# Parameter loads one chunk sooner, and the feed-forward block's last products a step sooner

## The chip, the core and the metric

The kernel runs on one core of a Trainium2 chip. The metric is the device time of one launch in microseconds. TensorE (PE in the rows, its weight loads PEld), VectorE (DVE), ScalarE (ACT) and GpSimd (POOL) each run their own instruction list in order; SyncE (SP) issues the DMAs. They meet at semaphores only.

## What is computed

Input x is 2048 tokens of 128 features. An attention layer, then a stack S0 of six layers, then a second attention layer, then the same stack again as S1 (same weights), each with a layer norm in front and added back to x. The change touches only the stacks:

```python
for i in range(DEPTH):                      # DEPTH = 6
    x = attn_layer(shift_tokens(x), Wqkv[i], q_scale[i], k_scale[i], Wo[i]) + x
    x = ffn_layer(shift_tokens(x), ln_g[i], ln_b[i], W1[i], b1[i], W2[i], b2[i]) + x

def ffn_layer(x, g, bln, W1, b1, W2, b2):
    xn = (x - mu) / jnp.sqrt(var + 1e-05) * g + bln
    hg = xn @ W1 + b1                       # W1: 128 x 682
    a, gate = jnp.split(hg, 2, -1)          # value and gate, 341 wide each
    return a * jax.nn.gelu(gate) @ W2 + b2  # W2: 341 x 128
```

`attn_layer` is attention over windows of 32 tokens with 16 heads of 64, normed and rotated queries and keys.

## The kernel before, in words

**Chunks, blocks, steps.** A stack cuts the 2048 tokens into 16 chunks of 128 (`NCH`). The feed-forward part works on blocks of 4 chunks (512 tokens, `NB` = 4 a layer). Every engine runs the same list of steps (`read_steps`): 16 steps for layer 0, a loop of 16 steps over layers 1 to 5, and a few steps that drain the pipeline (11 on PE, 12 on DVE). In step k an engine works on chunk k-d for several distances d: `at.chunk(d)`. `at.block(d)` gives block (k-d)//4 if (k-d) mod 4 is 3, so each piece of feed-forward work comes once in four steps. Steps with k beyond the layer reach back into the layer before. Each engine has its own step count: what DVE does with a chunk in its step k+2 answers what PE did with it in its step k. Below, "PE step 0, 1, 2, 3" is k mod 4 on PE.

**PE's step.** In this order: attention's output product (L602), transposition of the probabilities (L542), the query projection (L535 to L537) into `slot[0]`, probabilities times values (L681), scores (L704, L711) into `slot[3]`, transposition of the queries into `slot[2]` after `wait_for_slot2`, value projection, transposition of the attention output, key projection, transposition of the keys. Between them stands the feed-forward work of a block: mean (L669, `block(4)`, PE step 3), variance (L572, `block(5)`, step 0), the spread of the inverse deviation (L591, `block(6)`, step 1), three gate products (L546, `block(7)`, step 2), three value products (L546; `block(8)` in step 3, `block(9)` in step 0, `block(10)` in step 1) and the second product with W2 (L646, `block(11)`, step 2, ahead of the query projection). Value tile 1 lands in the half of `slot[2]` that the query transposition takes next, the second product in the half of `slot[3]` that the scores take next.

**The others.** ACT copies PE's outputs out of the slots and takes the Gelu of the gates (L862). DVE applies bias and gate to each value product (`hide`, L1155: three a block, by distances 9, 10, 11), does the norm's product (L1075, distance 7, which waits for all value products of the block before) and adds the second product, its bias and the residual into `XA` (L1118, distance 12, semaphore `f_done`). POOL does half of the rotation and the powers (L929, L913, L942, L946).

**Loads.** The stack's weights have one buffer each. SP's `layer` walks over the chunks c; per chunk it issues ten copies of the value windows (`window_values`, L456 to L460), which wait until ACT has copied the values of chunk c. Ahead of `window_values` of certain chunks it loads one parameter of this layer, after a wait that says that the layer before is through with the old one: `Wo` at c = 3, the rotation scales at 5, the norm's columns at 7, gate bias at 8, `W1` at 9, value bias at 10, `W2` at 11, `b2` at 12. Layers 1 to 5 of both stacks do this, ten times in all. The semaphores `wo_in`, `w1_in`, `value_b_in` release PE's L602 in step 4, PE's L546 in step 10 and DVE's first L1155.

Of the kernel before, what the change touches and what calls it, by code (L numbers as in the profile page):

```python
# [32 lines left out]
START = 1  # L33
# [57 lines left out]
def build(nc, A, out, place, stages=("A", "S0", "B", "S1")):  # L91
    n_const = A["shape_constants"].shape[1]
    ctx = ExitStack()
    with ctx:
# [153 lines left out]
        s = {n: sem(n) for n in names}  # L248
# [149 lines left out]
        def sp_stack(sp, call):  # L398
# [64 lines left out]
            def layer(L, following, after):  # L463
                first = isinstance(L, int) and L == 0
                g, f = L * NCH + CHUNKS * call, L * NB + BLOCKS * call
                t = (L + DEPTH * call) * 3
                if following is not None:
                    sp.wait_ge(s["w_lo_done"], START + t + 3)
                    load_q(following)
                for c in range(NCH):  # L470
                    if c == NCH - 1 and following is not None:
                        sp.wait_ge(s["w_lo_done"], START + t + 4)
                        load_v(following)
                        if after is not None:
                            sp.wait_ge(s["w_lo_done"], START + t + 5)
                            load_k(after)
                    if c == 3 and not first:
                        sp.wait_ge(s["y_mm"], START + g)
                        load_wo(L)
                    if c == 5:  # L480
                        sp.wait_ge(s["tables_done"], START + TABLES * call + 4 + 16 * L)
                        load_scales(0 if following is None else following)
                    if c == 7 and not first:
                        sp.wait_ge(s["ln_done"], START + norms_before(call) + f)
                        load_cols(L)
                    if c == 8 and not first:
                        sp.wait_ge(s["gelu_done"], START + 3 * f)
                        load_b1(L, 1)
                    if c == 9 and not first:
                        sp.wait_ge(s["value_mm"], START + 3 * f)  # L490
                        load_w1(L)
                    if c == 10 and not first:
                        sp.wait_ge(s["hid_done"], START + 3 * f)
                        load_b1(L, 0)
                    if c == 11 and not first:
                        sp.wait_ge(s["w2_mm"], START + f)
                        load_w2(L)
                    if c == 12 and not first:
                        sp.wait_ge(s["f_done"], START + 2 * f)
                        load_b2(L)  # L500
                    window_values(g, c)
# [25 lines left out]
        def pe_stack(pe, call):  # L527
            n0 = norms_before(call)
# [19 lines left out]
            def step(layer, g, f, k, lo, hi):  # L548
# [4 lines left out]
                def wait_for_slot2():  # L553
                    pe.wait_ge(s["ot_sb"], START + upto(k - 4))
                    pe.wait_ge(s["xb_done"], START + 2 * upto(k - 4))
                    if at.block(7) is not None:
                        pe.wait_ge(s["gelu_done"], START + 3 * blocks(k - 7))
                    if at.block(9) is not None:
                        pe.wait_ge(s["hid_done"], START + 3 * blocks(k - 9) - 1)
                    if at.block(10) is not None:  # L560
                        pe.wait_ge(s["hid_done"], START + 3 * blocks(k - 10))
                    if at.block(4) is not None:
                        pe.wait_ge(s["ln_centred"], START + n0 + blocks(k - 4))

# [71 lines left out]
                        pe.wait_ge(s["hid_done"], START + 3 * blocks(k - 11))  # L636
                    first_layer(slot[2][0:FT[2][1], 512:1024], 1, *FFN_TILES[2]).then_inc(s["gate_mm"], 1)

                b = at.block(11)
                if b is not None:  # L640
                    if b % NB == 0:
                        pe.wait_ge(s["w2_in"], START + 48 * (layer + DEPTH * call + b // NB + 1))
                    pe.wait_ge(s["hid_done"], START + 3 * (f + b + 1))
                    pe.wait_ge(s["sub_done"], START + upto(k - 3))
                    for t, (j, a, m) in enumerate(VALUE_TILES):
                        mm = pe.matmul(slot[3][:, 512:1024], W2[0:m, j, :], hidden[0:m, j, :],  # L646
                                       start=(t == 0), stop=(t == 2))
                    mm.then_inc(s["w2_mm"], 1)
# [7 lines left out]
                    pe.wait_ge(s["ak_done"], START + upto(c - 1))  # L656
                    project_in(slot[0], c % 4, 0).then_inc(s["q_mm"], 1)

                b = at.block(10)
                if b is not None:  # L660
                    pe.wait_ge(s["xb_done"], START + 2 * upto(k - 4))
                    if draining:
# [25 lines left out]
                if c is not None:  # L688
                    pe.wait_ge(s["qT_sb"], START + g + c + 1)
                    pe.wait_ge(s["kT_sb"], START + g + c + 1)  # L690
                    pe.wait_ge(s["sub_done"], START + upto(c - 1))
                    if at.block(5) is not None:
                        pe.wait_ge(s["ln_eps"], START + n0 + blocks(k - 5))
                    if at.block(6) is not None:
                        pe.wait_ge(s["ln_half"], START + n0 + blocks(k - 6))
                    if at.block(7) is not None:
                        pe.wait_ge(s["gelu_done"], START + 3 * blocks(k - 7))
                    if at.block(11) is not None:
                        pe.wait_ge(s["f_done"], START + 2 * blocks(k - 11))
                    if at.block(8) is not None:  # L700
                        pe.wait_ge(s["hid_done"], START + 3 * blocks(k - 8) - 2)
                    first = 0 if c % NCH == 0 else 1
                    for i in range(2):
                        pe.matmul(slot[3][:, i * 512:(i + 1) * 512], ident_b[:, :],  # L704
                                  mask_win[:, first:first + 1, :].to_broadcast([128, 8, 2 * WIN]),
                                  start=True, stop=False, skip_group_check=True)
                    for h in range(H):
                        r = 64 * (h % 2)
                        col = (h % 2) * 512 + (h // 2) * 64
                        for w in range(4):  # L710
                            mm = pe.matmul(slot[3][32 * w:32 * w + 32, col:col + 64],  # L711
                                           qT[r:r + 64, h // 2, 32 * w:32 * w + 32],
                                           kT[r:r + 64, h // 2, 32 * w:32 * w + 64],
                                           start=False, stop=True, skip_group_check=True)
                    mm.then_inc(s["s_mm"], 1)
# [35 lines left out]
                        pe.wait_ge(s["on_done"], START + upto(k - 3))  # L751
                    turn(slot[1], rot_out[1]).then_inc(s["tk_mm"], 1)

            read_steps(pe, call, step, 11)

        def act_stack(act, call):
            n0 = norms_before(call)
# [219 lines left out]
        def dve_stack(dve, call):  # L977
# [20 lines left out]
            def step(layer, g, f, k, lo, hi):  # L998
# [108 lines left out]
                    dve.tensor_tensor(rot_out[1][:, :], rot_out[1][:, :], rot_sin[1], ALU.add)\  # L1107
                       .then_inc(s["rk_done"], 1)

                b = at.block(12)  # L1110
                if b is not None:
                    if b % NB == 0:
                        dve.wait_ge(s["b2_in"], START + 16 * (layer + DEPTH * call + b // NB + 1))
# [10 lines left out]
                    dve.wait_ge(s["iq_done"], START + g + c + 1)  # L1124
                    normalise(0, "qn_done")

                b = at.block(11)
                if b is not None:
                    hide(layer, f, b, 2)

# [29 lines left out]
            for i, name in enumerate(names_of):  # L1160
# [1 line left out]
                                  const(name).rearrange("p (c d) -> p c d", d=DH),  # L1162
                                  qk_scales[:, i:i + 1, :].to_broadcast([128, NCH, DH]), ALU.mult)\
                   .then_inc(s["tables_done"], 1)
            read_steps(dve, call, step, 12)

            for b in range(NB):
                dve.wait_ge(s["f_done"], START + 2 * (BLOCKS * (call + 1) - NB + b + 1))
# [957 lines left out]
```

## Time and profile before

| | us |
|---|---|
| Time, median of 3 runs (7095.42 to 7106.72) | 7104.73 |
| The profiled execution's own time | 7119.09 |
| Its span | 7117.3 |
| Stack S0, first to last key copy of ACT (L821) | 1064.5 to 2984.9 |
| Stack S1, the same | 5129.3 to 7033.0 |

The profiled execution is 14.4 us above the median. Both stacks together are some 54% of the span. In the rows a line number is that of the kernel shown above, times are microseconds from the span's start, and an idle time in brackets is what the engine waited just before the group of instructions, with the instruction or DMA that ended the wait. One instruction serves as a marker of steps below: ACT's copy of the key projection, L821, once a step. From one L821 to the next is one step's length. Names of tiles that share memory are mixed in the rows: `W` is W1 or W2, `b` is a bias of the first product, and `normed<-slot,b,centred` is `hide`.

### The profile page before, as it was taken

How to read it: one execution, taken by the hardware profiler on the slowest of the kernel's cores; microseconds unless marked ns; L12 is line 12 of the kernel's file. 1: busy time of each engine (PE TensorE's matmuls, PEld its weight loads, DVE VectorE, ACT ScalarE, POOL GpSimd, SP SyncE). 2: the span in 40 equal slices, each digit the busy share in tenths (PEclk: the TensorE clock that was granted, in tenths of full speed). 3: DMA queues.
4: the chain of work that ended last, by engine and by line, in shares of the span. 5: the costliest groups of instructions: out<-in, count | busy, mean ns of one | idle time of the engine just before them, and what ended most of it. 6: DMA issues, size and time to landing. Idle time of an engine off the chain costs nothing. (4 is left out here: it accounts for less than half of the span.)

```text
span 7117.3 us, 188486 instructions
## 1 busy us (share of the span) xinstructions
PE 6050.2 (85%) x75387; PEld 4080.9 (57%) x75387; DVE 4642.6 (65%) x5380; ACT 3318.6 (47%) x3775; POOL 4252.9 (60%) x2000
## 2 busy tenths in 40 slices
PE   8989878888888888889889889999688888888887
PEld 4334436666666666655555555555376666666665
DVE  5425528887878887775455445543388787878776
ACT  1342246665656555513333333333366565656554
POOL 0000008777777777616567666667787777777764
PEclk6665569999999999989989989999899999999999
DMA  0000002222222222200000000000122222222221
GB/s 23 1 2 1 1 22 62 67 59 62 59 62 59 64 60 59 53 8 1 1 2 1 1 2 1 1 1 1 31 64 65 57 68 54 67 65 61 57 56 49
DMA packets 187287, 254.59 MB, mean 36 GB/s; under 512 B 59996, under 2 KB 80984, under 8 KB 186200
## 3 DMA queue, kind: packets, MB, share of 16 engines
q1 hardware_dynamic: 186392, 242.02, 13.1%
q8 instruction: 639, 10.47, 0.6%
q14 instruction: 256, 2.10, 0.1%
HBM read 38.98 MB, written 1.57 MB: 6 GB/s over the span
## 5 line engine op out<-in xcount | busy, mean ns | idle before, releaser
L1813 POOL TENSOR_TENSOR XB<-XB,Pb 128x1024 f32<-128x1024 f32 x448 | 1079.3, 2409 | 290.3 <-ACT Pb L1771 265.1
L913 POOL TENSOR_TENSOR sin_qk<-raw_qk,rot 128x512 f32<-128x512 f32 x768 | 1008.9, 1334 | 188.7 <-ACT raw_qk L875 133.1
L1865 DVE TENSOR_REDUCE b_pmax<-slot 128x1 f32<-128x1024 f32 x512 | 621.2, 1223 | 611.5 <-PE slot L1607 611.3
L1771 ACT ACTIVATE Pb<-slot 128x1024 f32<-128x1024 f32 x512 | 504.5, 1024 | 951.7 <-PE slot L1634 880.5
L946 POOL TENSOR_TENSOR inv_norm<-norm2c,minus_half 128x16 f32<-128x16 f32 x192 | 678.2, 3532 | 386.9 <-DVE norm2c L1088 386.9
L929 POOL TENSOR_TENSOR rot_out<-rot_out,sin_qk 128x1024 f32<-128x1024 f32 x192 | 601.2, 3131 | 337.7 <-DVE rot_out L987 336.6
L286 POOL TENSOR_TENSOR rstd<-variance,minus_half 128x4 f32<-128x4 f32 x20 | 19.8, 1008 | 1075.6 <-DVE variance L295 1075.5
L535 PE MATMUL slot<-w_hi,x_hi 128*128 128x512 f32 x1152 | 538.2, 467 | 73.5 <-POOL w_lo L904 43.4
L786 ACT ACTIVATE qT<-slot 128x1024 f32<-128x1024 f32 x192 | 197.1, 1026 | 794.3 <-PE slot L542 794.3
L942 POOL TENSOR_TENSOR inv_norm<-norm2c,minus_half 128x16 f32<-128x16 f32 x192 | 559.0, 2912 | 0.0
L987 DVE TENSOR_TENSOR rot_out<-slot,rot 128x1024 f32<-128x1024 f32 x384 | 467.9, 1219 | 83.5 <-PE slot L542 42.6
L711 PE MATMUL slot<-kT,qT 64*32 64x64 f32 x24576 | 334.6, 229 | 218.4 <-issue 218.3
L1644 PE MATMUL slot<-Pb,Vb 128*64 128x512 f32 x2048 | 494.3, 604 | 1.1 <-ACT Pb L1771 1.1
L542 PE MATMUL slot<-consts,rot_out 128*128 128x128 f32 x3072 | 435.1, 287 | 69.3 <-issue 39.5
L991 DVE TENSOR_TENSOR rot_out<-rot_out,inv_norm 128x1024 f32<-128x1024 f32 x384 | 474.9, 1237 | 6.8 <-POOL inv_norm L942 5.3
L602 PE MATMUL slot<-OT,Wo 128*128 128x128 f32 x3072 | 404.9, 288 | 82.7 <-DMA Wo<-in_Wo 80.0
L536 PE MATMUL slot<-w_lo,x_hi 128*128 128x512 f32 x1152 | 471.4, 409 | 2.6 <-issue 2.6
L537 PE MATMUL slot<-w_hi,x_lo 128*128 128x512 f32 x1152 | 469.6, 408 | 0.0
L711 PEld LDWEIGHTS slot<-kT,qT 64*32 64x32 f32 x24576 | 274.1, 107 | 325.9 <-issue 325.9
L602 PEld LDWEIGHTS slot<-OT,Wo 128*128 128x128 f32 x3072 | 386.5, 203 | 106.7 <-issue 101.8
L542 PEld LDWEIGHTS slot<-consts,rot_out 128*128 128x128 f32 x3072 | 363.8, 147 | 137.7 <-issue 84.0
L1632 PE MATMUL slot<-QA,KA 128*128 128x512 f32 x1024 | 423.6, 414 | 11.3 <-ACT Pb L1771 7.5
(223 smaller groups left out, 13525.8 us busy)
## 6 DMA issues: line engine op xcount, KB each, us to landing
VW<-V SPq DMA_DIRECT2D x1152, 128.0 KB
VW<-V SPq DMA_DIRECT2D x768, 64.0 KB
w_raw<-in_Wqkv SPq DMA_DIRECT2D x36, 512.0 KB, 3.6
Wo<-in_Wo SPq DMA_DIRECT2D x12, 512.0 KB, 4.1
W<-in_W SPq DMA_DIRECT2D x12, 341.0 KB, 3.1
consts<-in_shape_constants SPq DMA_DIRECT2D x1, 2436.5 KB, 8.7
W<-in_W SPq DMA_DIRECT2D x24, 64.0 KB
out<-out_nat SPq DMA_DIRECT2D x2, 512.0 KB, 3.4
```

The source lines that it names most:

```text
L535: pe.matmul(out, x_hi[ring][:, :], w_hi[:, cols], start=True, stop=False)
L542: mm = pe.transpose(o[:, j * 128:(j + 1) * 128], src[:, j * 128:(j + 1) * 128], ident)
L602: mm = pe.matmul(slot[2][:, 512:640], Wo[:, j, :], OT[:, j, :], start=(j == 0), stop=(j == 7))
L711: mm = pe.matmul(slot[3][32 * w:32 * w + 32, col:col + 64], qT[r:r + 64, h // 2, 32 * w:32 * w + 32], kT[r:r + 64, h // 2, 32 * w:32 * w + ...
L913: ins = pool.tensor_tensor(dst[:, :, x, :], src[:, :, 1 - x, :], tab, ALU.mult)
L929: pool.tensor_tensor(rot_out[0][:, :], rot_out[0][:, :], rot_sin[0], ALU.add)\
L942: pool.tensor_tensor(inv_norm[0][:, :], norm2c[0][:, :], minus_half[:, 0:H], ALU.pow)\
L946: pool.tensor_tensor(inv_norm[1][:, :], norm2c[1][:, :], minus_half[:, 0:H], ALU.pow)\
L1644: mm = pe.matmul(slot[3][64 * hh:64 * hh + 64, 0:512], Vb[:, k, :], Pb[:, n % B_RING, 512 * hh:512 * hh + 512], start=(k == 0), stop=(k == ...
L1771: act.activation(Pb[:, n % B_RING, :], slot[n % 2][:, :], ACT.Exp).then_inc(s["b_exp"], 1)
L1813: pool.tensor_tensor(b_sum[:, qb % 2, :], Pb[:, (n - 1) % B_RING, :] if k == 1 else b_sum[:, qb % 2, :], Pb[:, n % B_RING, :], ALU.add).th ...
L1865: dve.tensor_reduce(b_pmax[:, n // 2, n % 2:n % 2 + 1], o[:, :], AX.X, ALU.max).then_inc(s["b_max"], 1)
```

## The change

Every load of a layer's parameters moves one chunk up in SP's list. The value product of tile 1 moves from PE step 1 to PE step 0 of its block, with its `hide` on DVE one step sooner. The second product moves from PE step 2 to step 1, `f_done` one DVE step sooner. The waits of the slots follow. Both engines drain in one step less. No instruction is added or removed inside the layers; one wait is joined with another in `wait_for_slot2`, and one is added for the drain alone.

```diff
-                    if c == 3 and not first:
+                    if c == 2 and not first:
                         sp.wait_ge(s["y_mm"], START + g)
                         load_wo(L)
-                    if c == 5:
+                    if c == 4:
 ...                                             # scales
-                    if c == 7 and not first:
+                    if c == 6 and not first:
 ...                                             # norm columns; gate bias 8 -> 7
-                    if c == 9 and not first:
+                    if c == 8 and not first:
                         sp.wait_ge(s["value_mm"], START + 3 * f)
                         load_w1(L)
-                    if c == 10 and not first:
+                    if c == 9 and not first:
                         sp.wait_ge(s["hid_done"], START + 3 * f)
                         load_b1(L, 0)
-                    if c == 11 and not first:
+                    if c == 10 and not first:
                         sp.wait_ge(s["w2_mm"], START + f)
                         load_w2(L)
-                    if c == 12 and not first:
+                    if c == 11 and not first:
                         sp.wait_ge(s["f_done"], START + 2 * f)
                         load_b2(L)
@@ pe: wait_for_slot2
                     if at.block(9) is not None:
-                        pe.wait_ge(s["hid_done"], START + 3 * blocks(k - 9) - 1)
-                    if at.block(10) is not None:
-                        pe.wait_ge(s["hid_done"], START + 3 * blocks(k - 10))
+                        pe.wait_ge(s["hid_done"], START + 3 * blocks(k - 9))
@@ pe: second product
-                b = at.block(11)
+                b = at.block(10)
                 if b is not None:
+                    if draining:
+                        pe.wait_ge(s["ln_eps"], START + n0 + blocks(k - 6))
@@ pe: value product of tile 1
-                b = at.block(10)
+                b = at.block(9)
@@ pe: before the scores
-                    if at.block(11) is not None:
-                        pe.wait_ge(s["f_done"], START + 2 * blocks(k - 11))
+                    if at.block(10) is not None:
+                        pe.wait_ge(s["f_done"], START + 2 * blocks(k - 10))
-            read_steps(pe, call, step, 11)
+            read_steps(pe, call, step, 10)
@@ dve: f_done
-                b = at.block(12)
+                b = at.block(11)
@@ dve: third hide
-                b = at.block(11)
+                b = at.block(10)
                 if b is not None:
                     hide(layer, f, b, 2)
-            read_steps(dve, call, step, 12)
+            read_steps(dve, call, step, 11)
```

## Rows read from the trace of the kernel before

**Rows 1.** The page, part 1: busy time, share, instructions of each engine.

```profile
PE 6050.2 (85%) x75387; PEld 4080.9 (57%) x75387; DVE 4642.6 (65%) x5380; ACT 3318.6 (47%) x3775; POOL 4252.9 (60%) x2000
```

**Rows 2.** Waits, whole span: waiter <- releaser: us in total, times, longest.

```profile
PE slot L602 <- DMA Wo<-in_Wo: 80.0, 10, 8.2
PE slot L546 <- DMA W<-in_W: 60.8, 10, 6.3
DVE normed L1155 <- DMA b<-in_b: 40.6, 10, 4.5
DVE normed L1075 <- PE slot L546: 100.3, 46, 3.2
```

**Rows 3.** Timeline of SP's DMA issues, one layer: start, us, what.

```profile
2057.45 0.60 SPq L460 DMA_DIRECT2D VW<-V  x1
...
2078.84 0.40 SPq L422 DMA_DIRECT2D Wo<-in_Wo  x1
...
2199.74 0.59 SPq L460 DMA_DIRECT2D VW<-V  x1
...
2200.61 0.36 SPq L426 DMA_DIRECT2D W<-in_W  x1
...
2228.64 1.36 SPq L436 DMA_DIRECT2D b<-in_b  x3
```

**Rows 4.** Windows by step: length, busy (count) per engine, granted clock, DMA; sums.

```profile
sum 77.30, PE 55.06 PEld 41.09 DVE 50.12 ACT 37.19 POOL 45.63; mean PE 18.35 PEld 13.70 DVE 16.71 ACT 12.40 POOL 15.21
...
sum 59.90, PE 52.23 PEld 40.35 DVE 50.85 ACT 37.34 POOL 45.88; mean PE 17.41 PEld 13.45 DVE 16.95 ACT 12.45 POOL 15.29
...
6127.70:6155.10 27.40, 18.13 (x337) 14.63 (x336) 16.55 (x21) 10.62 (x13) 16.52 (x9) 0.81 0.22 60
...
sum 78.90, PE 55.23 PEld 41.49 DVE 49.47 ACT 37.20 POOL 44.60; mean PE 18.41 PEld 13.83 DVE 16.49 ACT 12.40 POOL 14.87
...
6211.10:6228.40 17.30, 15.44 (x337) 12.50 (x336) 16.50 (x21) 10.70 (x13) 15.93 (x9) 1.00 0.26 64
...
sum 55.80, PE 49.71 PEld 37.97 DVE 51.39 ACT 37.28 POOL 45.70; mean PE 16.57 PEld 12.66 DVE 17.13 ACT 12.43 POOL 15.23
```

**Rows 5.** Timeline of PE, output product after the wait for Wo, and in another step.

```profile
2082.83 3.78 PE L602 MATMUL slot<-OT,Wo 128*128 128x128 f32 x16 [7.88 <-DMA Wo<-in_Wo]
...
2179.14 1.95 PE L602 MATMUL slot<-OT,Wo 128*128 128x128 f32 x16
```

**Rows 6.** Timeline of PE in a PE step 1.

```profile
2183.45 1.02 PE L546 MATMUL slot<-normed,W 128*128 128x512 f32 x2
...
2189.77 1.09 PE L542 MATMUL slot<-consts,rot_out 128*128 128x128 f32 x8 [0.27 <-DVE normed L1155]
2191.10 0.50 PE L535 MATMUL slot<-w_hi,x_hi 128*128 128x512 f32 x1 [0.24 <-DVE Os L1142]
```

**Rows 7.** Timeline of a PE step 2: PE's second product and scores, ACT's Gelu.

```profile
2124.52 2.74 PE L646 MATMUL slot<-normed,W 128*128 128x512 f32 x6
2126.70 0.79 PE L535 MATMUL slot<-w_hi,x_hi 128*128 128x512 f32 x1
...
2130.28 0.60 PE L704 MATMUL slot<-mask_win,ident_b 128*128 128x512 bf16 x2 [0.21 <-issue]
...
2126.11 1.83 ACT L862 ACTIVATE centred<-slot,b 128x512 f32<-128x512 f32 x3
```

**Rows 8.** Timeline of a PE step 0: DVE's query normalisation, PE's query transposition.

```profile
2254.88 1.24 DVE L991 TENSOR_TENSOR rot_out<-rot_out,inv_norm 128x1024 f32<-128x1024 f32 x1
...
2257.60 1.09 PE L542 MATMUL slot<-consts,rot_out 128*128 128x128 f32 x8 [0.17 <-issue]
```

**Rows 9.** Timeline of the first stack's drain, DVE and PE.

```profile
3044.41 1.53 DVE L1118 SCALAR_TENSOR_TENSOR XA<-slot,ffn_cols,XB 64x512 f32<-64x512 f32 x2 [5.70 <-PE slot L646]
...
3046.09 2.81 PE L546 MATMUL slot<-normed,W 128*128 128x512 f32 x6 [1.72 <-DVE XA L1118]
```

**Rows 10.** View of one line, L1134: durations in ns, least, median, most.

```profile
L1134 DVE TENSOR_TENSOR x_lo<-XA,x_hi x192: 273/280/2332, 1053.7 to 7007.0; 128x128 fp32r<-128x128 f32 x192
```

More of the change, by code:

```diff
@@ L476, in layer @@
                             load_k(after)
-                    if c == 3 and not first:
+                    if c == 2 and not first:
                         sp.wait_ge(s["y_mm"], START + g)
                         load_wo(L)
-                    if c == 5:
+                    if c == 4:
                         sp.wait_ge(s["tables_done"], START + TABLES * call + 4 + 16 * L)
                         load_scales(0 if following is None else following)
-                    if c == 7 and not first:
+                    if c == 6 and not first:
                         sp.wait_ge(s["ln_done"], START + norms_before(call) + f)
                         load_cols(L)
-                    if c == 8 and not first:
+                    if c == 7 and not first:
                         sp.wait_ge(s["gelu_done"], START + 3 * f)
                         load_b1(L, 1)
-                    if c == 9 and not first:
+                    if c == 8 and not first:
                         sp.wait_ge(s["value_mm"], START + 3 * f)
                         load_w1(L)
-                    if c == 10 and not first:
+                    if c == 9 and not first:
                         sp.wait_ge(s["hid_done"], START + 3 * f)
                         load_b1(L, 0)
-                    if c == 11 and not first:
+                    if c == 10 and not first:
                         sp.wait_ge(s["w2_mm"], START + f)
                         load_w2(L)
-                    if c == 12 and not first:
+                    if c == 11 and not first:
                         sp.wait_ge(s["f_done"], START + 2 * f)
```

## The prediction

> **What bounds the kernel now.** I read the page first. PE is the busiest engine, 85% of the span [rows 1], but that is an average over stages, and the change touches only the stacks. So I read the waits next: who stands idle there, and what ends it. Three of the waits end on a DMA, and each comes exactly ten times, once for each layer that reloads its parameters: PE waits 80.0 us in all for `Wo`, 60.8 us for `W1`, and DVE 40.6 us for the value bias [rows 2]. A fourth wait of interest ends on PE: DVE's norm product waits 100.3 us for the value product of the block before [rows 2], 2.2 us in each of 46 blocks.
>
> Is it the issue or the transfer that is late? SP's timeline tells. `Wo` is issued at 2078.84 [rows 3], and PE's output product starts at 2082.83, after 7.88 us of idle time [rows 5]: 4.0 us from issue to use, so PE had stood still since 2074.95, before the load was even issued. SP could not issue sooner because the load stands behind the ten window copies of the chunk before, which in turn wait for that chunk's values. The same holds for `W1` (issued 2200.61) and the value bias (issued 2228.64) [rows 3].
>
> Then I ask what a step costs without the wait. The windows view, cut at ACT's L821, gives each step's length. I take the three steps with a DMA wait in one layer of each stack, and three steps of the same layer that do the same work (the same k mod 4, none with a wait for a load). First stack: 77.3 against 59.9 us, 17.4 us apart. Second stack: 78.9 against 55.8 us, 23.1 us apart [rows 4]. DVE and POOL are busy for about the same time in both (50.1 and 50.9 us DVE in the first pair), so the longer steps hold waiting, not work. In a clean step of 17.3 us PE is busy for 15.4, DVE for 16.5 and POOL for 15.9 us [rows 4]: three engines close to full. That is why I expect nothing below that length.
>
> **The loads, one chunk sooner.** No instruction is added. Each load now goes out behind the windows of a chunk earlier. For `Wo` that is right after 2057.45 + 0.60 = 2058.1 [rows 3], 20.8 us sooner, against 7.88 us that are missing. `W1` would go out one step sooner, 17.3 us if the step is a clean one [rows 4], against 60.8/10 = 6.1 us missing. The value bias takes the place that `W1` has now, 28.0 us sooner [rows 3], against 4.1 us. All three waits go, with over 10 us to spare.
>
> What each wait on SP holds up: behind it stand the ten window copies of the next chunk, and behind those PE's L681. But these copies wait for the values of the next chunk in any case, which PE makes late in the following step, and what the loads wait for has happened by then: each of the old parameters is last read in the step in which SP gets there or before, since `value_mm`, `hid_done`, `w2_mm` and `f_done` themselves come a step sooner. I take 0 for this; if one wait held SP, it would have to hold it for over 10 us before PE saw it.
>
> What comes back: the whole difference between the pairs of steps, since that is measured between steps with and without the wait. Mean (17.4 + 23.1)/2 = 20.25 us a layer, times 10: **-202 us**, with 174 and 231 us as bounds. It is more than PE's idle time, and a row shows why. After the wait for `Wo` the sixteen matmuls of L602 take 3.78 us, otherwise 1.95 us [rows 5], and the granted clock of that kind of step is 0.81 on average against 1.00 in the clean one [rows 4]: for part of the step PE runs at the lower of its two levels (1.2 instead of 2.4 GHz) right after having been idle. So a removed wait also takes the slow matmuls behind it away.
>
> The Trainium skill, "TensorE: Matmul & The Clock Gate", Part 1, puts it so: the throttled state is the default and activity releases it. By this the extra is part of the gain. If it were not, only the waits themselves would return, some 18.1 us a layer and 181 us in all; the clock in the rows agrees with the page.
>
> **The feed-forward products, a step sooner.** Work only moves, so I price each of four PE steps by what comes and goes. A value product costs 1.02 us (L546 x2) [rows 6]. The second product takes from 2124.52 to 2126.70, and the matmul behind it takes 0.79 instead of 0.50 us [rows 6, 7], which gives 2.18 + 0.29 = 2.47 us.
>
> - PE step 0 gains the value product: **+1.02**. New wait: the query transposition now also needs the third `hide`, 0.75 us of DVE, which stands right behind DVE's query normalisation. In the rows that normalisation ends at 2256.12 and PE gets to the transposition at 2257.60 [rows 8], so `hide` ends at 2256.9 and costs nothing. Without this cover it would cost 0.75 us, and behind it in PE's list is all the rest of the step.
> - PE step 1 gains the second product and loses the value product, +2.47 - 1.02. The `hide` that left it had PE wait 0.27 us, and the attention output behind it 0.24 us more [rows 6]; both go: **+0.94**. New wait: the scores now need `f_done` here, 1.53 us of DVE [rows 9] ahead of the query normalisation. It can start when the second product is done; PE has the query projection and L681 (some 3 us) to do meanwhile, so I take 0. DVE's step grows by 1.53 and shrinks by 0.75 and by the 2.2 us wait for the value product.
> - PE step 2 loses the second product. PE then gets to the scores 2.47 us sooner, but they also wait for the Gelus, which end at 2126.11 + 1.83 = 2127.94, against 2130.28 now [rows 7]: **-2.34**. What is late next there is ACT, then DVE, which loses `f_done` in this step.
> - PE step 3: nothing.
>
> Sum -0.38 us for four steps, times 46 blocks: **-17 us**. Bounds: if the `hide` wait is paid in full and nothing of step 1's waits returns, +1.77 + 1.45 - 2.34 = +0.88, times 46 = +40 us. If the added work fills waits that PE has anyway in steps 0 and 1 (it is busy for 15.4 us of the 17.3 us of a clean step [rows 4], so there are 1.9 us to fill), only the -2.34 stays: -108 us. I take the middle value, as its terms are read from rows of the very steps.
>
> **The drain.** In the last steps of a stack PE's value products wait 1.72 us for DVE's `f_done` of the block before, which waited for the second product [rows 9]. That product now lies ahead of the gates. About 2 us a stack: **-4 us**; between 0 and -5.7 each, the idle time of DVE there.
>
> **Sum.** -202 - 17 - 4 = -223 us. Against the profiled execution's own 7119.1 us that is 6896 us. It lies 14.4 us above the median, so the median should be 7104.7 - 223 = **6881 us**.
>
> **The rivals.**
> 1. *The waits go, but less comes back* (0.15). Another engine is late where the load was. For it: in the first stack's pair the clean steps are no shorter than 59.9 us, and three engines are nearly full. Price: 174 back, +40 for the products, -4: -138, so 6967 us.
> 2. *The products bring more* (0.08). DVE's wait of 100.3 us goes from a path on which POOL waits for it: -231 - 108 - 4 = -343, so 6762 us. Against it: PE has more to do in that very step.
> 3. *DVE and POOL collide more often* (0.06). DVE's 128x128 subtraction L1134 takes 0.28 us as a rule and up to 2.33 us [rows 10], although nothing in it changes. If the new order adds (0.28 + 2.33)/2 - 0.28 = 1.0 us of this in two steps of each block, 2 x 46 x 1.0 = 94 us are lost: 6975 us. The Trainium skill, "SBUF — State Buffer", names a cause: a port pair shared by VectorE and GpSimd, held by one of them for a whole instruction. The rows show the long durations, not the cause.
> 4. *Slower* (0.04). The moved work lies in series on both engines and step 2 gives nothing back: the PE work and the DVE work each lengthen their steps, 2.47 + 1.02 + 0.75 + 1.53 = 5.77 us a block, times 46 = 265 us against 206 us of loads and drain: +59, so 7164 us. The place is PE's wait for `f_done` ahead of the scores in step 1. It decides from 206/46 = 4.5 us a block on. Against it: rows 7 and 8 show cover for two of the four terms.
> 5. *It does not do what it says* (0.03): SP gets to the loads sooner, but is held there until the old time. Only the drain moves: 7101 us, no change. Against it: the copies ahead of `W1` end at 2199.74 + 0.59 = 2200.33, and it follows at 2200.61 [rows 3], so the place in SP's list decides, not the semaphore.
>
> **How the numbers follow.** The forecast has 0.60; its own range is 6840 to 6935 us (174 to 231 us of loads, and half of the way to the bounds of the products). The remaining 0.04 is for gains of another size. The range that should hold the time 8 times in 10 takes in the forecast and rivals 1 and 3: 6825 to 6985 us. Differences below 0.2% (14 us) can't be told from none here. Faster: 0.60 + 0.15 + 0.08 + 0.06 + 0.04 = 0.93. Same: 0.03. Slower: 0.04.
>
> **What would show it.** The three DMA waits of rows 2 gone from the list, and the steps that held them as long as their like, near 17, 21 and 18 to 22 us. L602 near 1.95 us in each step 4. A second product in PE step 1, with that step about 1 us longer and PE step 2 over 2 us shorter. DVE's L1075 without its wait. Wrong would be: a long wait of PE's L704 for L1118 (rival 4), or of L542 for L1155 in PE step 0 (rival 1), an SP wait ahead of a load (rival 5), or steps with the load now bound by POOL or DVE at over 20 us.

## The result and the profile after

The changed kernel takes 6796.92 us (median of 4 runs, 6793.93 to 6798.29) against 7101.05 us of the kernel before beside it. The ratio is 0.9571 with a 95% interval of 0.9555 to 0.9588: 304 us or 4.3% faster. 223 us were forecast, with a range of 6825 to 6985 us. The direction is right; the gain is 81 us larger, and the time lies 28 us below the range.

The page of the changed kernel, the row that answers to [rows 1], and two of the page's groups of instructions:

```profile
PE 5957.6 (88%) x75387; PEld 4031.7 (59%) x75387; DVE 4574.7 (67%) x5380; ACT 3310.4 (49%) x3775; POOL 4234.6 (62%) x2000
...
L946 POOL TENSOR_TENSOR inv_norm<-norm2c,minus_half 128x16 f32<-128x16 f32 x192 | 668.9, 3484 | 171.4 <-DVE norm2c L1088 171.1
...
L600 PE MATMUL slot<-OT,Wo 128*128 128x128 f32 x3072 | 389.5, 281 | 2.7 <-ACT OT L814 2.7
```

The counts are the same. PE has 92.6 us less busy time with the same 75387 matmuls: some of them ran faster, as matmuls behind a long wait had been slow [rows 5]. The output product alone went from 404.9 to 389.5 us. It is now L600 and waits for nothing but 2.7 us of ACT, where 80.0 us stood [rows 2]. DVE's wait of 100.3 us for the value product [rows 2] is gone from the list of waits, and its wait for the second product went from 157.8 to 14.3 us. POOL's wait for DVE at L946 was 386.9 us in the page of before and is 171.1 now.

SP's timeline in the layer of [rows 3]:

```profile
1983.17 0.59 SPq L460 DMA_DIRECT2D VW<-V  x1
1984.04 0.40 SPq L422 DMA_DIRECT2D Wo<-in_Wo  x1
...
2096.15 0.36 SPq L426 DMA_DIRECT2D W<-in_W  x1
```

The windows of the three steps that held a wait for a load (length, busy per engine, granted clock, DMA share, GB/s), and their sum:

```profile
1998.90:2015.30 16.40, 15.96 (x339) 12.83 (x338) 15.54 (x21) 10.66 (x13) 15.38 (x9) 1.00 0.25 66
2108.10:2126.20 18.10, 16.09 (x333) 12.39 (x332) 14.29 (x18) 13.66 (x17) 14.67 (x8) 1.00 0.25 61
2126.20:2145.10 18.90, 15.46 (x331) 12.03 (x329) 16.67 (x22) 12.91 (x16) 14.05 (x8) 1.00 0.26 67
...
sum 53.40, PE 47.51 PEld 37.25 DVE 46.51 ACT 37.24 POOL 44.09; mean PE 15.84 PEld 12.42 DVE 15.50 ACT 12.41 POOL 14.70
```

`Wo` goes out 0.3 us after the last window copy, so SP holds it for nothing. The three steps are 53.4 us long instead of 77.3 [rows 4], at the full clock.

To see where the rest came from I take the distance between the L821 markers in every step, as a mean over layers 1 to 5 of both stacks, and group the sixteen steps of a layer by PE's k mod 4. The distance from marker i to marker i+1 holds PE step i+1; behind the last marker of a stack there is none, so the step that begins a layer is a mean of eight and not of ten. All values in the table below come so from the trace of the kernel named, in us a step:

| kernel | PE step 0 | PE step 1 | PE step 2 | PE step 3 | a block | time to before |
|---|---|---|---|---|---|---|
| before | 21.75 | 18.17 | 22.90 | 20.04 | 82.9 | 1 |
| all loads sooner | 19.28 | 18.85 | 20.40 | 19.25 | 77.8 | 0.9718 |
| loads, value product | 19.25 | 18.03 | 20.16 | 19.16 | 76.6 | 0.9639 |
| the whole change | 19.30 | 19.23 | 17.96 | 19.06 | 75.5 | 0.9576 |

(The last two rows are of runs e12 and e15 below, which ran on one chip.) The loads shorten PE step 0 (`Wo`), PE step 2 (`W1`) and PE step 3 (the value bias). The products shorten step 2 and lengthen step 1 by little.

### The profile page after: what moved, and what is told of

Its sections match the earlier page's. It is cut to its first block and busy times, and to the rows that moved or that the text cites. A ratio compares the mean times of both kernels' runs of the same rounds, so it can differ in the third digit from the quotient of the medians.

```text
span 6792.1 us, 188444 instructions
## 1 busy us (share of the span) xinstructions
PE 5957.6 (88%) x75387; PEld 4031.7 (59%) x75387; DVE 4574.7 (67%) x5380; ACT 3310.4 (49%) x3775; POOL 4234.6 (62%) x2000
## 5 line engine op out<-in xcount | busy, mean ns | idle before, releaser
L946 POOL TENSOR_TENSOR inv_norm<-norm2c,minus_half 128x16 f32<-128x16 f32 x192 | 668.9, 3484 | 171.4 <-DVE norm2c L1088 171.1
L711 PE MATMUL slot<-kT,qT 64*32 64x64 f32 x24576 | 333.1, 228 | 182.0 <-issue 181.8
L1634 PE MATMUL slot<-QB,KB 66*128 66x512 f32 x1024 | 416.3, 407 | 0.0
L600 PE MATMUL slot<-OT,Wo 128*128 128x128 f32 x3072 | 389.5, 281 | 2.7 <-ACT OT L814 2.7
```

The source lines that it names most:

```text
L600: mm = pe.matmul(slot[2][:, 512:640], Wo[:, j, :], OT[:, j, :], start=(j == 0), stop=(j == 7))
L711: mm = pe.matmul(slot[3][32 * w:32 * w + 32, col:col + 64], qT[r:r + 64, h // 2, 32 * w:32 * w + 32], kT[r:r + 64, h // 2, 32 * w:32 * w + ...
L946: pool.tensor_tensor(inv_norm[1][:, :], norm2c[1][:, :], minus_half[:, 0:H], ALU.pow)\
```

## The experiments

**Loads or products.** All eight loads alone, the products alone, the value product alone, and `Wo` alone.

```diff
 e1_loads: all eight "if c == n" lines as in the change, nothing else
 e2_products: all of the change but the loads
 e3_value:
-                b = at.block(10)          # pe: value product of tile 1
+                b = at.block(9)
-                b = at.block(11)          # dve: third hide
+                b = at.block(10)
 e4_wo:
-                    if c == 3 and not first:
+                    if c == 2 and not first:
                         sp.wait_ge(s["y_mm"], START + g)
                         load_wo(L)
```

> The kernel before with all eight loads a chunk sooner and nothing else. The whole change took 304 us off. Theory A, the sum on record: the loads bring 202 us (bounds 174 and 231), so about 6899 us. Theory B: the loads bring nearly all of it, 280 us or more, about 6820 us or less, because a wait for a load held back more steps than the one in which it stood. Either way the three DMA waits are gone.

Measured: 6927.14 us, ratio 0.9718 (0.9702 to 0.9735), which is 200 us off. Theory A holds to 2 us, theory B falls. In the markers the three steps that had waited are 22.8 us a layer shorter, more than the 20.25 us forecast, and the other thirteen are 2.5 us longer; 2.7 us of this is the step after marker 4. SP now waits in one place, 11.6 us in all and 1.7 us at most, ahead of `W1`.

> The kernel before with the load of Wo alone a chunk sooner. By the pairs of steps on record (10.4 us in the first stack, 10.1 us in the second) 102 us, about 6999 us. By the bare wait of the trace, 80 us, about 7021 us. If more than the one step gains, over 110 us.

Measured: 7028.69 us, ratio 0.9862 (0.9844 to 0.9879), 98 us off. The pairs of steps had priced it at 102 us, the bare wait at 80 us, which lies outside the interval (86 us at its near end). The pair method is the better one.

> The kernel before with the value product, the third hide, the second product and the addition a step sooner, and the loads where they were. The sum on record gives 21 us (17 + 4), so about 7080 us. Theory C: the products bring some 100 us, about 7000 us, because DVE's wait of 100.3 us for the value product was on a path that POOL waited for. Theory B says 7080 us or more.

Measured: 7055.03 us, ratio 0.9888 (0.9867 to 0.9909), 80 us off. The sum on record (21 us) is refuted; theory C's 100 us are nearer, though the next run shows that its reason carries only a part. Together with the loads the products bring more still: 0.9718 to 0.9571, 104 us.

> The kernel before with the value product of tile 1 and its hide alone a step sooner; second product, addition and loads stay. It takes away DVE's wait for the value product (100.3 us) with no other work moved. Theory C: some 100 us faster, about 7000 us. The sum on record, by its terms: PE step 0 gains 1.02, step 1 loses 1.02 + 0.27 + 0.24, so 0.5 us a block or 23 us faster, about 7078 us.

Measured: 7066.01 us, ratio 0.9918 (0.9902 to 0.9935), 58 us off, between the two theories (23 and 100 us). The step that the value product left, PE step 1, is 1.1 us shorter (18.17 to 17.04 us), the one that took it in 0.2 us longer.

**Where a product on PE is free.** To price PE work by itself I added products of constants whose result is overwritten.

```diff
 e7_dummy0: loads sooner, and in PE step 0 behind the query projection
+                b = at.block(9)
+                if b is not None:
+                    pe.wait_ge(s["xb_done"], START + 2 * upto(k - 4))
+                    pe.matmul(slot[2][:, 512:1024], const("centre128"), const("rot_q_cos")[:, 0:512],
+                              start=True, stop=True)
 e11_dummy0_late: the same product behind the scores
                     wait_for_slot2()
+                    if at.block(9) is not None:
+                        pe.matmul(slot[2][:, 512:1024], ...)
                     turn(slot[2], rot_out[0]).then_inc(s["tq_mm"], 1)
 e8_dummy1: loads sooner, and in PE step 1 ahead of the query projection
+                b = at.block(10)
+                if b is not None and not draining:
+                    pe.wait_ge(s["sub_done"], START + upto(k - 3))
+                    for t in range(3):
+                        pe.matmul(slot[3][:, 512:1024], ...)
```

> The kernel with all loads sooner (0.9718 of before) and one more product of 128x512 on PE in step 0 of every block, at the place that the value product moves to; it multiplies constants and its result is overwritten. The price on record is 1.02 us a block in full, 47 us: 0.9784. Theory D, such work is hidden in step 0: 0 to 15 us, 0.9718 to 0.974.

Measured: 6910.52 us, ratio 0.9703 (0.9679 to 0.9727). The product costs nothing in PE step 0 (19.26 us against 19.28 without it); 1.02 us a block had been charged, 0.9784, which lies outside the interval.

> All loads sooner and one more product of 128x512 in PE step 0, as in the run in which it cost nothing (0.9703 against 0.9718 without it), but behind the scores instead of ahead of them. Theory H: ahead of L681 and L711 the product fills time in which PE would have stood still inside these two groups for no wait that the profile shows (1.9 us a step without it, 1.1 us with it); behind them it can't, and costs 0.86 to 1.02 us a block, 40 to 47 us: 0.977 to 0.978. Rival: the step is bound by DVE and POOL, and the product is free at either place: 0.970 to 0.973.

Measured: 6945.47 us, ratio 0.9759 (0.9743 to 0.9776). The same product some 6 us later in the same step costs 0.56% more than ahead (40 us, though the two ran on different chips). Against no product it costs 0.41%, 29 us, or 0.66 us in PE step 0; theory H had charged 40 to 47 us, which the intervals don't rule out. Being free hangs on the place. The timeline of PE in the same step of the same layer shows it, first without the product, then with it ahead (L662), then with it behind (L722):

```profile
6078.34 1.66 PE L681 MATMUL slot<-VW,probsT 64*32 64x64 f32 x128
6080.05 0.60 PE L704 MATMUL slot<-mask_win,ident_b 128*128 128x512 bf16 x2
6080.58 1.12 PE L711 MATMUL slot<-kT,qT 64*32 64x64 f32 x91
6083.88 0.63 PE L711 MATMUL slot<-kT,qT 64*32 64x64 f32 x37 [2.18 <-issue]
```

```profile
6082.20 1.02 PE L662 MATMUL slot<-consts 128*128 128x512 f32 x2
6083.15 1.48 PE L687 MATMUL slot<-VW,probsT 64*32 64x64 f32 x128
6084.72 0.60 PE L710 MATMUL slot<-mask_win,ident_b 128*128 128x512 bf16 x2
6085.26 0.84 PE L717 MATMUL slot<-kT,qT 64*32 64x64 f32 x63
6087.22 0.86 PE L717 MATMUL slot<-kT,qT 64*32 64x64 f32 x65 [1.12 <-issue]
```

```profile
6088.46 1.61 PE L681 MATMUL slot<-VW,probsT 64*32 64x64 f32 x128
...
6093.43 0.78 PE L711 MATMUL slot<-kT,qT 64*32 64x64 f32 x55 [1.78 <-issue]
6094.33 1.12 PE L722 MATMUL slot<-consts 128*128 128x512 f32 x2
```

"Issue" marks idle time in which PE waits for nothing that the profile shows. It stands in the middle of the 128 short matmuls of the scores. From the start of the values' product (L681, L687) to the end of the scores it is 6.17 us without the extra product and 4.93 us with it ahead: 1.24 us shorter, more than the 0.95 us that the product takes up in PE's row. As a mean over the 30 such steps that don't begin a layer it is 5.73 us without the product, 4.78 us with it ahead and 5.27 us with it behind. The last value warns: up to the end of the scores e11 has the same instructions as e1, and yet is 0.46 us shorter, so not all of the 0.95 us is the product's doing.

The same 30 steps show what gave way. With the product ahead PE is busy for 0.43 us more, not 0.95, while the mean granted clock rises from 0.97 to 1.00, so the other matmuls ran a little faster; and PE is idle for 0.63 us less. With the product behind, it is 0.76 us more and 0.30 us less. The prediction's bound of -108 us had this as added work that "fills waits that PE has anyway".

What PE stands still for inside these groups can be read from the DMA packets in the trace. Queue 8 carries packets of 16384 bytes of the kind "instruction"; the page of e1 has them as

```profile
q8 instruction: 639, 10.47, 0.7%
```

In e1 PE stands still 182 times for over 0.6 us inside the values' product or the scores. In 180 of these it goes on 1.2 to 1.6 us after such a packet has landed, 1.38 us in the median; of random moments in the stacks 6% lie so. In the three stops above the packet lands at 6082.39, 6085.72 and 6092.01, and PE goes on at 6083.88, 6087.22 and 6093.43. So PE waits for its instructions there. In the first of them the packet sets out 0.4 us after the scores have begun, in the second, with the product ahead, 0.5 us before. What decides when a packet sets out was not tested.

> The kernel with all loads sooner and three more products of 128x512 on PE in step 1, ahead of the query projection, where the second product moves to; results overwritten, none in the drain. In full 2.47 us a block for 44 blocks: 109 us, 0.987. Theory D, partly hidden: 1.2 to 2.0 us a block, 53 to 88 us, 0.979 to 0.984.

Measured: 7013.64 us, ratio 0.9854 (0.9824 to 0.9884), 97 us more than without, above theory D's 53 to 88 us but by less than the intervals. In PE step 1 the work is nearly paid in full, 2.2 of 2.47 us, although it stands ahead of the short matmuls here too: being ahead of them is not enough. Two rows from the waits of this kernel say how it travels; the same two of the kernel with the loads alone follow:

```profile
DVE normed L1082 <- PE slot L546: 212.1, 46, 5.3
POOL inv_norm L953 <- DVE norm2c L1095: 356.0, 153, 6.5
```

```profile
DVE normed L1075 <- PE slot L546: 97.8, 46, 2.8
POOL inv_norm L946 <- DVE norm2c L1088: 247.5, 147, 4.9
```

DVE waits in its norm's product for the value product, 2.5 us a block longer, and POOL's power behind it waits as much longer. So as long as the value product stands in PE step 1, PE work ahead of it delays DVE and, through DVE, POOL. With the loads in place the value product's move alone takes POOL's wait from 247.5 to 169.7 us (e12 below).

**The second product.**

> All loads a chunk sooner, and the value product of tile 1 with its hide a step sooner; second product and addition stay. Loads alone were 0.9718 of before, the value product alone 0.9918, the whole change 0.9571. If the two add, 0.9636, and the second product brings the last 0.65% (46 us), where the sum on record had it cost 2.47 - 2.34 = 0.13 us a block, 6 us. Theory D, the work moved into PE steps 0 and 1 is hidden there: the steps with k mod 4 = 0 stay at about 17.3 us. If the second product brings nothing, this kernel is at 0.957.

Measured: 6845.82 us, ratio 0.9614 (0.9591 to 0.9636), 74 us below the loads alone.

> All loads sooner and the value product a step sooner (0.9614 of before), with three more products of 128x512 in PE step 1 ahead of the query projection, the cost of the second product without its gain in step 2. With the value product still in step 1 three such products cost 1.36%, 97 us, and DVE's wait for the value product grew from 2.2 to 4.9 us a block. Theory G: that wait is what carries PE's delay on to POOL, and once the value product is gone from the step, the same work costs what the second product does in the changed kernel, 0.84 us a block: 37 us, 0.9666. Rival: PE's work in that step is paid in full anyway, 2.2 us a block: 97 us, 0.975, and the second product is cheap for another reason.

Measured: 6931.56 us, ratio 0.9750 (0.9732 to 0.9768). By the medians of two chips 97 us were paid, which speaks for the rival. By the two traces it is 43 us (spans 6870.5 and 6913.7), but the traced execution of e5 was the slowest of its four and that of e9 the fastest of its five, so this figure is worth little. To settle it, base, cost alone, gain alone and the whole change ran on one chip:

```diff
 e12: loads and value product sooner           e15: the changed kernel
 e13: e12 and three products of constants in PE step 1, as in e8
 e14: e12 with the second product left out
-                    for t, (j, a, m) in enumerate(VALUE_TILES):
-                        mm = pe.matmul(slot[3][:, 512:1024], W2[0:m, j, :], hidden[0:m, j, :], ...)
+                    mm = pe.matmul(slot[3][:, 512:1024], ident_b[:, :],
+                                   ident_b[:, :].unsqueeze(1).to_broadcast([128, 4, 128]), start=True, stop=True)
```

> All loads and the value product sooner, once more, as the base on the same chip for the next three: 0.9614 of before, as measured.

> The base with three more products in PE step 1, on the same chip as the base. Theory G: 0.84 to 1.04 us a block, 37 to 46 us over the base, 0.967 to 0.968. Rival: paid in full, 2.2 us a block, 97 us, 0.975.

> The base without the second product: in its place in PE step 2 stands one short bf16 product, so 2.2 of 2.47 us of PE time are gone from step 2 (the sum with W2 is left out, the addition on DVE stays). The sum on record has step 2 gain 2.34 us a block, 108 us, because the scores then wait for the Gelus: 0.946. If no such cover is met, 2.2 us or less a block, 101 us, 0.947. If other engines hold the step up, 1 us a block, 46 us, 0.955.

> The whole change on the same chip: 0.957 of before. Theory G with the gain on record gives the base less (2.34 - 0.84) x 46 = 69 us, 0.952. The rival (cost in full) gives 2.34 - 2.2 = 0.1 us a block, 0.961.

| kernel | median us | ratio | over e12 | PE step 1 | PE step 2 | the other two |
|---|---|---|---|---|---|---|
| e12, base | 6865.78 | 0.9639 (0.9621 to 0.9658) | | 18.03 | 20.16 | 38.41 |
| e13, cost alone | 6936.54 | 0.9742 (0.9723 to 0.9760) | +71 | 19.31 | 20.02 | 39.05 |
| e14, gain alone | 6796.81 | 0.9548 (0.9529 to 0.9566) | -69 | 17.76 | 18.23 | 39.05 |
| e15, both | 6816.59 | 0.9576 (0.9557 to 0.9596) | -49 | 19.23 | 17.96 | 38.36 |

Step 1 pays 1.28 us in e13 and 1.20 us in e15 for work that takes 2.47 us on PE by [rows 6, 7]: about half. Step 2 gains 1.9 us in e14 and 2.2 us in e15; 2.34 us were forecast. The two steps agree with each other and with theory G's direction. The times fit neither side of what was expected: e13's 71 us lie half way between theory G (37 to 46 us) and its rival (97 us), and e14's 69 us between 46 and 101 us. Nor do they add: +71 - 69 = +2, measured -49 us. The steps say where the 51 us lie. PE steps 0 and 3, which have no edit, are 0.64 us a block longer in e13 and in e14 alike, 1.3 us together or 59 us in 46 blocks, and this is not so in e15. In e14 one of them differs between two copies of the same instructions: from marker 3 to 4 of the layer it is 17.2 us in the first stack and 19.5 us in the second. Which stop of this kind grows when the list of instructions changes, I can't predict; that part stays open.

How half of the work in step 1 is hidden can be read from the windows of its 40 steps, e12 against e15. PE is busy for 15.40 and 17.23 us: 1.83 us more, not 2.47, at a mean granted clock of 0.93 and 0.98. It is idle for 2.63 and 2.00 us, and its stops inside the values' product and the scores fall from 2.12 to 1.42 us. So one part fills stops in which PE waited for instructions, and in the other PE's remaining work ran faster, with more of the step at the upper level of the clock. ACT's wait for the query projection (L875) goes from 78.4 to 158.8 us with the second product ahead of it.

**Place within the step.**

```diff
 e10_behind: the changed kernel, second product behind the query projection
+                c = at.chunk(0)
+                if c is not None: ...     # query projection
                 b = at.block(10)
                 if b is not None: ...     # second product
-                c = at.chunk(0)
-                if c is not None: ...
```

> The changed kernel with the second product behind the query projection in PE step 1, not ahead of it. Theory G: what is left of its cost (0.84 us a block) comes from the late query copy (ACT waits 2.9 us for it in that step against 0.4): up to 0.8 us a block faster, 37 us, 0.952. Rival: the addition on DVE is then late for the scores (it ends 1.4 us later), and nothing is won or 20 us are lost, 0.957 to 0.960.

Measured: 6822.14 us, ratio 0.9590 (0.9570 to 0.9609): 0.9571 and 0.9576 were measured for the change as it is. No gain; the rival's side. PE step 1 is as long with either order (19.19 and 19.23 us). ACT's wait for the query projection falls from 158.8 to 49.9 us, and nothing comes of it.

**The rotation scales.** One step of the changed kernel got longer, the one after marker 4, from 17.7 to 21.1 us. The loads alone do that too (20.4 us), `Wo` alone by 1.2 us, so the scales are most of it and not all.

```diff
 e6_scales5: the changed kernel with
-                    if c == 4:
+                    if c == 5:
                         ...
                         load_scales(0 if following is None else following)
```

> The changed kernel with the rotation scales loaded at c = 5 again. In the changed kernel the step after key copy 4 is 21.1 us long against 17.7 before, and the one after key copy 5 17.0 against 20.6. Theory S, these six loads lengthen whichever step they are issued in by about 3 us: the two steps change places and the time stays within 10 us. Rival: only their new place hurts, the step at 4 falls to 18.5 and the one at 5 stays at 17: 25 us faster.

Measured: 6822.47 us, ratio 0.9577 (0.9549 to 0.9605), the same as the change within the intervals. The windows of the two steps, changed kernel first, then this one:

```profile
2318.70:2340.30 21.60, 18.37 (x340) 14.64 (x339) 16.28 (x21) 11.22 (x14) 14.91 (x8) 0.92 0.23 56
2340.30:2357.30 17.00, 16.00 (x333) 12.34 (x332) 14.19 (x18) 13.66 (x17) 14.54 (x8) 1.00 0.26 65
```

```profile
2329.60:2348.00 18.40, 17.11 (x341) 13.32 (x340) 16.06 (x21) 11.22 (x14) 14.79 (x8) 1.00 0.23 60
2348.00:2368.90 20.90, 17.20 (x333) 13.53 (x332) 14.42 (x18) 13.61 (x17) 14.71 (x8) 0.92 0.24 58
```

The length moves with the load. The longer of the two has the lower granted clock both times, 0.92, so some of it is slower matmuls behind the stop. In both kernels PE stands still in the scores a few us after SP has issued these six DMAs. Changed kernel, SP and PE, then the run with the scales at 5:

```profile
2023.71 0.86 SPq L417 DMA_DIRECT2D qk_scales<-in_k_scale  x2
...
2029.53 1.39 PE L711 MATMUL slot<-kT,qT 64*32 64x64 f32 x79 [2.86 <-issue]
```

```profile
2356.52 0.91 SPq L417 DMA_DIRECT2D qk_scales<-in_k_scale  x2
...
2362.04 0.89 PE L711 MATMUL slot<-kT,qT 64*32 64x64 f32 x39 [3.00 <-issue]
```

Here too PE goes on 1.5 us after an instruction packet has landed (2028.04 and 2360.54). The packets take 0.9 us, no longer than others (1.0 us in the median); they set out late, some 0.4 to 0.6 us after PE has stopped. Why they do behind these six DMAs was not tested.

## Why the prediction was right in its larger part and wrong in its smaller

**The loads: right in place and mechanism, in size with some luck.** -202 us forecast, -200 us measured (e1); for `Wo` alone 102 and 98 us. The three waits are gone, SP is held for 1.7 us at most (e1) and in the changed kernel not at all, and the slow matmuls behind the wait went with it, as the pairs of steps had it. That the sum met the time to 2 us is partly luck: the three steps gave 22.8 us a layer and not 20.25, and 2.5 us were lost in the others. Most of that is the step after marker 4, which the scales now lengthen. In the changed kernel this costs nothing in sum, because they had lengthened the next step before (e6); with the loads alone the next step is only 1.0 us shorter for 2.7 us. Nor was 17.3 us the floor that I took it for: the `Wo` step above is 16.4 us long.

**The value product in PE step 0: the step that failed.** +1.02 us a block was charged in full. I had read the clean step as 15.4 us of PE work in 17.3 us and had named the filling of these 1.9 us as one end of the range, but took the full price, on the ground that the term was read from a row. The term's duration was right; that it lies on the path was not shown by any row. The steps with the value product are no longer than those without (19.25 against 19.28 us). e7 shows the same for a product of constants, and e11 that it hangs on the place: in this step PE work ahead of the two groups of short matmuls was free, behind them it cost 0.66 us. Ahead it shortened the stops for instructions and kept the clock up. The `hide` wait in that step cost nothing, as forecast.

**PE step 1: charged +0.94, measured +0.38** (18.85 to 19.23 us). It is made of two wrong terms. The value product's leaving brought 0.82 us where 1.53 was forecast, and the second product cost 1.20 us where 2.47 was. The DVE wait that I left without a price (2.2 us a block) mattered: e8 shows that with it in place work in this step goes on to POOL. Once the value product is gone about half of the second product fits in: PE's idle time in that step falls by 0.63 us, and its busy time grows by 1.83 us and not by 2.47, at a higher granted clock. The forecast's rule, that moved work costs what its rows say, has neither.

**PE step 2: right.** -2.34 forecast, -2.2 us measured in e15 against e12, -1.9 with the work simply left out (e14, whose time fell by 69 us and not by 101, because other steps grew).

**The sum of the products.** Forecast -0.38 us a block, -17 us. From the loads alone to the whole change the table gives 77.77 - 75.54 = 2.23 us a block, times 46 = 103 us, and the times 104 us. The difference to the forecast, 1.85 us a block, is 1.0 in step 0, 0.6 in step 1 and 0.2 in step 3, where nothing was edited, and 0.1 in step 2.

**The drain.** -2 us a stack forecast. In the first stack the time from the last marker to DVE's final addition (L1170) is 3054.20 - 2984.85 = 69.35 us before and 2887.51 - 2823.04 = 64.47 us after: 4.9 us. In the second stack it is 69.94 and 67.17 us: 2.8 us. Both are over the forecast and within the bound of 5.7.

**The range.** It was too narrow at the low end: the bound of -108 us for the products was known and priced, and at most half of the way to it was let in. The sum was not even carried through. By its own words, 231 us of loads and half of the way from -17 to -108, the forecast's range begins at 7104.7 - 231 - 45.5 - 17 - 4 = 6807 us and not at 6840, and the outer one began above that, at 6825. The measured time lies below 6807 too. Rival 2 joined the bound to the upper bound of the loads and so came out at 6762 us, with a chance of 0.08. With the loads at their own value it would have been -202 - 108 - 4 = -314 us, 6791 us, which is 6 us from what was measured. Rival 2's reason, DVE's wait on a path on which POOL waits, is borne out by e8 and e12; its size is not. Rivals 4 and 5 did not happen: PE's wait for `f_done` ahead of the scores is 5.1 us in the whole span, and SP gets to the loads in time. Rival 1 fell with e1. Rival 3 would have made the kernel slower than forecast, which it is not; no run looked at it by itself.

**The clock.** With the wait gone, the granted clock of the `Wo` step shown above is 1.00 instead of 0.81, and 98 us came back for 80 us of wait. Of the two readings in the prediction (extra part of the gain, or waits only) e4 decides for the first, by 98 against 80 us. The Trainium skill, "TensorE: Matmul & The Clock Gate", Part 1, where activity releases the throttle, agrees.

## What to carry to other kernels

Price a wait for a load by a pair of steps with the same work, one with and one without the wait: that gave 202 for 200 us, since it holds the slow matmuls behind the wait too. Before you charge moved work in full, look in the step that receives it for stops of that engine behind the new place, and at the granted clock; a step in which each engine is 90% busy can still take a microsecond for nothing. Add such work by itself, with constants, before you believe either price: the same place in two kinds of step gave free and nearly full. And where one engine waits for a product that is in no hurry itself, look at what stands behind that wait on the waiting engine: here the value product held DVE's norm and, through it, POOL. Last, carry a range's sum through, and let in the bounds that you have priced.

## What the runs showed of the hardware that I had not expected

- In a run of 128 short matmul pairs PE stands still for 1 to 3 us with no wait in the profile. Of the 182 stops over 0.6 us in the values' product and the scores of e1, 180 end 1.2 to 1.6 us after a 16384-byte instruction packet has landed, and so do 146 of 150 in the changed kernel: PE runs short of instructions there, not of data. For the line of the scores the time without a wait in the profile comes to 241.3 us in e1 and 181.8 us in the changed kernel, so fewer or shorter stops are part of what the products brought.
- Six small loads (768 pieces of 128 to 256 bytes) on SP's queue lengthen the step by 2.5 to 3.5 us, although PE waits for none of them. Moved by a chunk, the stop moved along (e6), and it too ends 1.5 us after an instruction packet. The packet is late and not slow; how the six DMAs make it late is open.
- The same steps in the two stacks, and the same steps of kernels with small differences, differ more than the forecast assumed: the step from marker 1 to 2 of the changed kernel is 17.1 us in the first stack and 20.6 us in the second. The medians of two kernels on different chips were 97 us apart; on one chip they were 71 us apart.
